# The first two head pairs of an attention stage scored straight from an fp32 projection, with the operand stacks of that block written by one queue

## What is computed

```python
qkv = x @ w_qkv.T                    # x is layer-normalised, 16 heads of 8 channels
q, k, v = (_split_heads(t) for t in jnp.split(qkv, 3, axis=-1))
L = jnp.einsum('bhqd,bhkd->bhqk', q, k) * scale
k_y = _split_heads(x @ w_ky.T)
L_y = jnp.einsum('bhqd,bhkd->bhqk', q, k_y) * scale
agg = jnp.sum(jnp.exp(jnp.clip(L_y, -15.0, 15.0)) * mask, axis=-1, keepdims=True) + EPS
r = jnp.log(jnp.abs(L) + EPS) - jnp.log(agg + EPS)
w = jax.nn.softplus(r) * mask
A = w / (jnp.sum(w, axis=-1, keepdims=True) + EPS)
out = jnp.einsum('bhqk,bhkd->bhqd', A, v)     # then the output projection and the residual
```

## Time before, and the profile of one execution

| | us |
|---|---|
| median of 3 executions | 423.61 |
| lowest and highest | 421.04, 424.43 |
| span of the profiled execution | 421.1 |

### The profile page before, as it was taken

One profiled execution on the slowest core, in us unless ns is written; L12 is line 12 of the kernel. 1 busy time (PEld: TensorE's weight loads), 2 busy tenths in 40 slices (PEclk: granted clock), 3 DMA queues, 4 the chain that ended last, 5 costly groups with the idle time before them and its releaser, 6 DMA issues.

```text
span 421.1 us, 8327 instructions
## 1 busy us (share of the span) xinstructions
PE 330.0 (78%) x2412; PEld 195.9 (47%) x2412; DVE 304.9 (72%) x628; ACT 297.8 (71%) x866; POOL 149.6 (36%) x252
## 2 busy tenths in 40 slices
PE   6878899995766435778788677777978996889992
PEld 6638899752233111222334223242333473589992
DVE  5653443378899969999999999988999657444431
ACT  2915456424999979999999989996777646345561
POOL 5575544400443560021411214112530016654452
PEclk9989999996699655876958969878998989899997
DMA  8775666134478996001200012000300274666540
GB/s 248 263 222 153 199 162 173 46 107 138 133 203 224 220 243 134 0 2 38 64 0 2 0 39 63 2 2 0 101 0 2 66 264 121 189 189 180 166 134 26
DMA packets 37993, 47.61 MB, mean 113 GB/s; under 512 B 4288, under 2 KB 26816, under 8 KB 37696
## 3 DMA queue, kind: packets, MB, share of 16 engines
q1 hardware_dynamic: 33616, 36.20, 31.7%
q0 software_dynamic: 2560, 6.30, 5.3%
q10 hardware_dynamic: 1776, 4.60, 3.3%
HBM read 24.02 MB, written 6.29 MB: 72 GB/s over the span
## 4 chain that ended last, share of the span: by engine, by line
ACT 34%; PE 33%; DVE 13%; issue 6%; DMA 4%; POOL 3%; SPq 2%; DVEq 1%; another core or an unknown queue 1%; ACTq 1%; POOLq 0%
ACT R L944 14%; PE PS L1522 9%; ACT R L952 9%; PE PS L1532 8%; ACT CL L944 7%; PE PS L1667 3%; PE PS L1451 3%; PE PS L1475 2%; SPq L463 2%; DVE R L1296 2%; DVE R L1281 2%; DMA QPS<-R 2%; PE PS L1649 2%; DVE R L1027 1%; ACT R L969 1%
## 5 line engine op out<-in xcount | busy, mean ns | idle before, releaser
L1296 DVE TENSOR_TENSOR R<-PS,MB 128x1024 int32<-128x1024 int32 (+1 forms) x96 | 97.9, 1034 | 13.3 <-PE PS L1649 13.1
L836 ACT ACTIVATE R<-PS,R 128x128 f32<-128x128 f32 x184 | 52.6, 368 | 49.1 <-PE PS L1522 23.8
L952 ACT ACTIVATE R<-R 128x1024 f32<-128x1024 f32 x64 | 80.0, 1261 | 9.7 <-DVE R L1296 9.6
L944 ACT ACTIVATE R<-R 128x384 f32<-128x384 f32 (+2 forms) x192 | 77.1, 411 | 3.1 <-DVE R L1281 3.1
L1634 PE MATMUL PS<-R 64*128 64x512 bf16 (+3 forms) x256 | 40.1, 367 | 33.7 <-DVE CL L1281 16.3
L1281 DVE SCALAR_TENSOR_TENSOR R<-PS,MA 128x1024 f32<-128x1024 f32 x64 | 59.5, 946 | 1.1 <-PE PS L1634 1.1
L1667 PE MATMUL PS<-R,V 128*32 128x256 f32 (+3 forms) x512 | 56.3, 526 | 3.6 <-ACT R L952 3.5
L1522 PE MATMUL PS<-R 128*128 (+1 forms) x368 | 51.7, 283 | 6.2 <-DVE R L1162 4.5
L1649 PE MATMUL PS<-QPS,R 64*128 64x512 bf16 (+3 forms) x256 | 38.2, 349 | 15.5 <-DVE R L1281 8.4
L1522 PEld LDWEIGHTS PS<-R 128*128 128x128 f32 x368 | 44.6, 191 | 10.2 <-issue 8.5
L1532 PE MATMUL PS<-R 128*128 (+1 forms) x368 | 48.8, 276 | 0.7 <-ACT R L836 0.7
(11 more groups left out here) (184 smaller groups left out, 460.8 us busy)
## 6 DMA issues: line engine op xcount, KB each, us to landing
R<-w SPq DMA_DIRECT2D x38, 258.0 KB
R<-R SPq DMA_DIRECT2D x32, 128.0 KB, 2.4
R<-R SPq DMA_DIRECT2D x16, 256.0 KB, 7.9
QPS<-R SPq DMA_DIRECT2D x32, 128.0 KB, 2.4
R<-w ACTq DMA_DIRECT2D x8, 258.0 KB
rows_d<-X SPq DMA_DIRECT2D x8, 256.0 KB, 3.9
R<-w ACTq DMA_DIRECT2D x1, 2048.0 KB, 8.3
rows_d<-R SPq DMA_DIRECT2D x8, 256.0 KB, 2.4
```

Of the source, the lines that this page charges most:

```text
L836: last = act.activation(HT[:, k % 2, c * P:(c + 1) * P], PS[:, k % 2, c * P:(c + 1) * P], ACT.Gelu, bias=W1[:, k, F + c:F + c + 1])
L944: act.activation(e, e, ACT.Exp, scale=SCALE, accum_out=aggf[:, ds(s + (2 * i + par) * STEPS, 1)])\
L952: act.activation(w, w, ACT.Ln, bias=1.0, scale=1.0).then_inc(s_ln, 1)
L1296: dve.tensor_tensor(weights(v)[:, :, at:at + n].bitcast(i32), PS[:, SLOTS[slot(b_fill(v, g))], 0:n].bitcast(i32), spread(mask, 1, 2), ALU. ...
```

## The change

**Direct scores.** Two more projections of block 0, with weights WS, give queries and `k_y` keys of the first four head pairs' worth of rows spaced so that head (pair, parity) has its 8 rows at partition 0, 32, 64 or 96. WS is cleared by POOL and filled from WA in the first expert layer, where WH was made. ScalarE copies the queries out of PSUM (`direct_queries`), VectorE the keys (`direct_keys`), both in fp32, into FS, and steps 0 and 1 (DIRECT = 2) are scored by fp32 matmuls with 8 rows instead of bf16 ones with 64. TensorE waits at step 0 for these two copies and for the stacks only at step 2.

**Stacks.** WH, `half_stack` and `first_keys` go; the first two stacks are written whole by SyncE, 16 DMAs of 128 KB, in the order first terms, second terms, third terms.

**Engines.** The second terms of m = 0 and 1 go from ScalarE to POOL. The normalised rows of blocks 1 to 3 go from VectorE to POOL (`middle_rows`, 12 instructions), with most of their inverse deviations. The copies of the turned blocks 1 to 3 go from ScalarE to VectorE.

**Order.** Projection 2 goes behind step 1, 3 inside step 2, 4 behind step 2, then one a step (`PROJECT_AT`); the turns of blocks 1, 2, 3 behind steps 1, 3, 4 (`TURNS_AT`), with banks 7, 7, 7; the token-major rows t = 0 to 7 behind steps 1, 2, 3, 5, 5, 6, 7, 7 (`ROWS_AT`). On VectorE remainders, copies and `value_rows` stand between the clips of a step (`between`), not behind them. On POOL terms of m = s + 1 are made in step s, where it was s + 2.

```diff
+DIRECT = 2
+FIRST_BANK = (6, 7)
+PROJECT_AT = (None, None, 1, None, 2, 3, 4, 5, 6, 7, 8, 9)
+ROWS_AT = (1, 2, 3, 5, 5, 6, 7, 7)
+TURNS_AT = {1: 1, 2: 3, 3: 4}
-TURN_BANK = ((0, 1, 0, 1), (0, 1, 0, 7), (7, 7, 0, 1))
+TURN_BANK = ((0, 1, 0, 1), (0, 7, 7, 7), (7, 7, 0, 1))
...
-            half_stack(0, 0)
-            half_stack(1, 0, (2,))
-            for i in range(2):
-                half_stack(i, 1)
+            for term in range(TERMS):
+                for i in range(2):
+                    stack(i, (term,))
...
+            def middle_rows(b):
+                for n in range(b * TB, (b + 1) * TB):
+                    pool.tensor_scalar(XN2[:, n, :], X[:, n, :], mv[:, n, 0:1], lnt[:, 2, n:n + 1],
+                                       ALU.subtract, ALU.mult).then_inc(s_xn, 1)
...
-                m = s - 1 + FIRST_PROJECTIONS
-                if s == 1:
-                    second_term(2)
-                    third_term(2)
-                if 0 < s < A_AT:
+                m = s + 1
+                for k in {1: (2,), 3: (3, 4)}.get(s, (m,) if 3 < s < A_AT else ()):
+                    second_term(k)
+                    third_term(k)
+                if s == A_AT:
                     second_term(m)
-                    third_term(m)
-                elif s == A_AT:
-                    second_term(m)
-                elif s == R_AT:
+                elif s in (R_AT, Q_AT):
                     third_term(m - 1)
                     second_term(m)
-                elif s == Q_AT:
+                elif s == Q_AT + 1:
                     third_term(m - 1)
                     second_term(m)
                     third_term(m)
...
+                if s == 2 and g == 0:
+                    remainder(2)
+                if s == 3 and g < 2:
+                    remainder(3 + g)
+                if g == 0 and 4 <= s < len(PROJECTIONS) - 1:
+                    remainder(s + 1)
+                for b in range(1, NB):
+                    if g == 0 and s == TURNS_AT[b] + 1:
+                        copy_xnt(b)
+                for t in range(NT // 2):
+                    if s == ROWS_AT[t] + 1 and g == (2 if t in (4, 7, 1) else 1):
+                        value_rows(t)
...
+            def bank_read(t):
+                pe.wait_ge(s_qc, t + 1)
+                pe.wait_ge(s_vc, 2 * t + 2)
...
+                if k == 1 and g == 2:
+                    bank_read(1)
+                if k == 1 and g == 3:
+                    pe.wait_ge(s_xnt, NB + 3)
...
+            def direct_projections():
+                for w in range(2):
+                    pe.matmul(PS[:, FIRST_BANK[w], :], WS[:, w, :], XNT2[:, 0:SEQ],
+                              start=True, stop=True).then_inc(s_pe, 1)
...
-                if b == NB - 1:
+                if b:
+                    pe.wait_ge(s_xnt, NB + b + 1)
...
+                        if s < DIRECT:
+                            rows = slice(QUAD * (s % 2 * 2 + par), QUAD * (s % 2 * 2 + par) + HD)
+                            last = pe.matmul(to, FS[rows, 0, i * P:(i + 1) * P],
+                                             FS[rows, 1, 0:(i + 1) * P], start=True, stop=True)
```

More of the change, by code:

```diff
@@ L355, in build @@
         s_den = sem("denominators_summed")
+        s_ilin = sem("middle_inverse_deviation_begun")
         s_linv = sem("last_inverse_deviation_begun")
@@ L756, in normalise @@
                                    ALU.mult).then_inc(s_num, 1)
+            def middle_rows(b):
+                for n in range(b * TB, (b + 1) * TB):
+                    pool.tensor_scalar(XN2[:, n, :], X[:, n, :], mv[:, n, 0:1], lnt[:, 2, n:n + 1],
+                                       ALU.subtract, ALU.mult).then_inc(s_xn, 1)
+            var, inv, tmp = (lnt[:, k, TB:] for k in (0, 2, 3))
+            pool.wait_ge(s_ilin, 1)
+            link(pool.tensor_tensor(tmp, inv, inv, ALU.mult))
+            link(pool.tensor_tensor(tmp, tmp, var, ALU.mult))
+            link(pool.tensor_scalar(tmp, tmp, -0.5, 1.5, ALU.mult, ALU.add))
+            link(pool.tensor_tensor(inv, inv, tmp, ALU.mult))
+            for m in range(2):
+                second_term(m)
+            for b in range(1, NB):
+                middle_rows(b)
             for s in range(END_STEP):
@@ L1265, in _ @@
             variance(3)
-            remainder(0)
-            inverse(3)
-            remainder(1)
-            for m in range(2):
-                last_term(m)
-            normal_rows(3, XN2)
+            direct_keys()
+            dve.wait_ge(s_std, 4)
+            dve.reciprocal(lnt[:, 2, TB:], lnt[:, 1, TB:]).then_inc(s_ilin, 1)
             def clip_scores(s, g):
@@ L1344, in after @@
                         scaled_q_terms(b)
-                m = s - 1 + FIRST_PROJECTIONS
-                if s == 1:
-                    remainder(2)
-                    dve.wait_ge(s_c, 9)
-                    for t in range(FIRST_ROWS):
-                        v_rows(t)
-                if s and m < len(PROJECTIONS):
-                    remainder(m)
-                if FIRST_ROWS < s <= NT // 2:
-                    v_rows(s - 1)
                 for b in range(NB):
@@ L1385, in between @@
             def between(s, g):
+                if s == 0 and g < 2:
+                    remainder(g)
+                if s == 0 and g == 2:
+                    for m in range(2):
+                        last_term(m)
+                if s == 2 and g == 0:
[4 more added lines that the diff above has]
+                    remainder(s + 1)
+                for b in range(1, NB):
+                    if g == 0 and s == TURNS_AT[b] + 1:
+                        copy_xnt(b)
+                for t in range(NT // 2):
+                    if s == ROWS_AT[t] + 1 and g == (2 if t in (4, 7, 1) else 1):
+                        value_rows(t)
                 for b in range(NB):
@@ L1605, in _ @@
             pe.wait_ge(s_xnt, NB + 1)
-            pe.wait_ge(s_wh, 2)
+            pe.wait_ge(s_wsp, 2)
+            direct_projections()
             for m in range(2):
                 project(m)
-            for t in range(FIRST_ROWS):
-                q_v_rows(t)
-            project(2)
-            for b in range(1, NB - 1):
-                turn(1, b)
-            pe.wait_ge(s_xnt, 2 * NB - 1)
-            pe.wait_ge(s_c, 9)
+            pe.wait_ge(s_c, 8)
             def slot_free(n):
@@ L1701, in after @@
             def after(s):
-                if s != 1 and s + FIRST_PROJECTIONS < len(PROJECTIONS):
-                    project(s + FIRST_PROJECTIONS)
-                if s == 2:
-                    pe.wait_ge(s_qc, 2)
-                    pe.wait_ge(s_vc, 4)
-                    turn(1, NB - 1)
-                if FIRST_ROWS <= s < NT // 2:
-                    q_v_rows(s)
+                for m in range(2, len(PROJECTIONS)):
+                    if s == PROJECT_AT[m]:
+                        project(m)
+                for b in range(1, NB):
+                    if s == TURNS_AT[b]:
+                        turn(1, b)
+                for t in range(NT // 2):
+                    if s == ROWS_AT[t]:
+                        q_v_rows(t)
                 if s == NT // 2 + 1:
-                    pe.wait_ge(s_qc, NT // 2)
-                    pe.wait_ge(s_vc, NT)
+                    bank_read(NT // 2 - 2)
+                    bank_read(NT // 2 - 1)
                 for b in range(NB):
@@ L1742, in _ @@
                 if s == 0:
-                    for i in range(2):
-                        pe.wait_ge(s_stk0[i], STACK_DMAS)
-                if s == HP // 2:
+                    pe.wait_ge(s_eq, 1)
+                    pe.wait_ge(s_ek, 1)
+                if s == DIRECT:
                     for i in range(2):
```

111 lines of the change are left out of this document (52 added, 59 removed).

## The result

| | before | changed |
|---|---|---|
| median of the runs, us | 422.53 (421.04 to 424.43, 4 runs) | 434.15 (433.17 to 438.08, 4 runs) |
| span of the profiled execution, us | 421.1 | 432.6 |
| first turn of block 0 in it, us | 89.62 | 91.45 |

The ratio is 1.0294, with a 95% interval of 1.0252 to 1.0337: about 12 us slower, where 433.0 (425 to 440) and "slower" with 0.85 were forecast. The forecast stood on a median of 423.6 for the kernel before; one more execution brought that to 422.53. As a difference, 9.4 us were forecast and 11.6 measured.

The account below looks back on a forecast made before the run. ScalarE's gapless 4.36 us steps, after a fixed chain to step 0, were taken to bound the kernel. Step 2 came earlier, later waits outweighed it: +9.5 at the second logarithm, 433 us, range 425 to 440.

Parts of the forecast that it names:

- Step 0: Start of the attention: with direct fp32 scores, step 0's exponentials start at 97.4, 6.1 us earlier.
- Step 2: Its start waits for the 16 stack DMAs, landing at 107.8: 109.4 to 109.6 instead of 112.9.
- Step 2 to 3: Projection 3 waits for VectorE's copy of block 1, projections 3 and 4 at half clock: 8.1 us.
- 3 to 4: VectorE's remainders, clips and value rows 1 hold up the turn of block 2: 6.8 us.
- 4 to 5 and 5 to 6: Remainder and copy delay clip 1, 5.3 us; then remainder 6, copy, projection 7 and token-major rows, 5.9 us.
- rival 1: TensorE stays at 1.2 GHz longer: +13.3 (437) through step 4, +21 (444) through step 7; chance 0.17.
- 6 to 9: Steps of 5.0, 5.0 and 5.1 us, with clip 1 late and two query rows in the first two.
- 9 to 12: Remainders 10 and 11 wait for POOL's third terms; step 9 at 150.6, step 10 at 157.8, step 11 at 163.9.
- The idle time before the first logarithm: ScalarE's old idle of 2.11 us there goes, since the scaled queries land while ScalarE is still busy.
- Rival 2: Only the two remainders behind POOL's new order cost, steps 2 to 8 keeping 4.36 us: +1.7, 425; chance 0.10.
- rival 4: The fp32 scores take the time the stacks took, leaving step 2 where it was: 436; chance 0.03.
- Rival 3: Faster: issue time hides, stacks land by 105.5, step 2 follows step 1 at 106.6: 417.3; chance 0.05.

Follow-up runs that it names:

- e10: Changed kernel with the edits of e1, e7 and e8 together (POOL order, ScalarE copies, VectorE work behind the third clip); 427.84 us, ratio 1.0125 to the kernel before.
- e2: Changed kernel plus idle bf16 products on TensorE in steps 0 to 2, meant to keep its clock up; ratio 1.0307 to the kernel before.
- e7: Changed kernel with the copies of turned blocks 1 to 3 given back from VectorE to ScalarE; ratio 1.0195 to the kernel before.
- e6: As e4, without the idle products of steps 0 and 1 and with projection 11 behind the turn of the scaled queries; ratio 0.996 to the kernel before.
- e1: Changed kernel with only POOL's order around the last two remainders altered, terms made earlier; ratio 1.0195 to the kernel before.
- e11: As e6, but the first turned scaled queries go to PSUM bank 6 instead of 7; ratio 0.9943 to the kernel before.
- e9: Changed kernel with the edits of e1 and e7 together; 426.90 us, ratio 1.0084 to the kernel before.
- e8: Changed kernel with VectorE's remainders and value rows put behind the third clip, copies left between clips; ratio 1.0345 to the kernel before.
- e4: Changed kernel's start plus idle products in steps 0 and 1, with later work back in the old kind of order, a step ahead; ratio 1.0017 to the kernel before.
- e3: Changed kernel with both the idle products of e2 and the POOL order of e1; ratio 1.0305 to the kernel before.

## Why the prediction came out as it did

The mechanism was right in nearly every step, and the sum of the stage was 2.3 us short: +9.5 forecast at the second logarithm, +11.8 measured. That 433.0 and 434.15 lie only 1.2 us apart owes something to luck: the base of the forecast was 1.1 us higher than the median that it was compared with. And the forecast let the shift go through to the end, where the profiled executions give back 1.8 us behind the last exponentials. By its own steps:

- **Step 0.** Forecast 97.4, that is 7.8 behind the turn; measured 7.56. The unknown price of the fp32 scores was put at 1.0 us for 512 columns, which makes 2.5 for a step; a step's 16 passes took 1.99 + 0.70 us at full clock and 4.78 at half. Right.
- **Step 2.** Forecast 109.4 to 109.6, 19.8 to 20.0 behind the turn, bound by the stacks; measured 20.64. The reason held, by a hair. The last of the 16 DMAs was issued 10.0 us after the first, where 9.75 was taken, and landed 2.3 to 2.6 us later, where 2.1 was taken; that is most of the 0.8 us. TensorE waited only 0.24 us for it, because the clock had fallen at about 100.2, while step 0 ran, and not in the idle time behind step 1 as forecast: all of step 1's work on TensorE went at half clock and ended at 110.11. That the landing bound the step shows in e10, where TensorE was done 0.5 us sooner, stood still for 0.72 us and began the scores at the same 18.90 us behind the turn:

```profile
108.69 0.61 PE L1663 MATMUL PS<-R 64*128 64x512 bf16 x6 [0.72 <-issue]
```

- **Step 2 to 3.** 8.1 forecast, 7.78 measured, with the copy, the idle TensorE (2.41) and projection 3 behind it in the order given. e2 (6.19 at full clock) and e7 (5.36 with the copy gone) confirm both halves.
- **3 to 4.** 6.8 forecast, 6.53 measured.
- **4 to 5 and 5 to 6.** 5.3 and 5.9 forecast, 6.04 and 7.47 measured. This is the term that was too small, by 2.3 us together. The sum had full clock from here on, since the old trace had it from 113 on the earlier trace rows; in the changed kernel it fell again. Projection 6 took 2.05 us, projection 7 1.46, and the two sets of token-major rows 3.26 where 3.0 was meant to hold them and projection 7. Stretches of the changed kernel, columns as above:

```profile
126.00:128.00 2.00, 0.57 (x3) 0.41 (x4) 2.00 (x4) 1.34 (x4) 0.89 (x2) 0.88 0.78 208
128.00:130.00 2.00, 2.00 (x5) 0.86 (x5) 1.69 (x4) 1.27 (x6) 0.88 (x1) 0.50 0.74 199
130.00:133.00 3.00, 1.61 (x11) 0.54 (x9) 1.82 (x3) 2.29 (x11) 0.00 (x0) 0.84 0.74 200
133.00:138.00 5.00, 4.25 (x10) 2.86 (x10) 2.33 (x4) 4.01 (x18) 1.77 (x2) 0.66 0.43 120
```

  It is rival 1 in part: not half clock through step 7, but in three stretches of it, about 114 to 117, 127.5 to 131 and 134.5 to 138. That TensorE's new gaps let it fall is what the runs suggest (with e6's order it stays full from step 2 to step 9), not a thing that one of them isolates.
- **6 to 9.** 5.0, 5.0 and 5.1 forecast; 4.94, 5.15, 4.85 measured. Clip 1 comes 0.5, 0.5 and 0.3 us late for ScalarE there; the second set of query rows in step 7 and 0.33 us ahead of step 9's first exponential are most of the rest.
- **9 to 12.** 7.2 and 6.1 forecast, 7.25 and 6.24 measured, with VectorE idle for 2.38 and 2.00 us where 2.2 and 2.0 were expected. The idle time before the first logarithm is gone, as forecast. e1 shows that the order was worth 3.5 us.
- **Rival 2** (only the two remainders cost) and **rival 4** (the fp32 scores eat the gain of step 0) are out: rival 2 by the table, rival 4 by step 0 at 7.56. **Rival 3** (faster) named the wrong condition. It wanted the stacks down at 105.5, with the rest of the order as the change has it. What makes this start pay is the order of the steps (e6, e11), and then it pays 0.4 to 0.6%. With earlier stacks and the new order TensorE's half clock would have held step 2 to within 0.24 us all the same.

What the forecast missed as an idea: it priced each in-step wait for itself, at one clock. Two terms do add up (e1 and e7 in e9). The others aren't independent: moving VectorE's work back alone gave nothing up to step 8 (e8), on top of e9 it gave nothing either (e10), and with TensorE's schedule moved back as well all of the loss up to step 9 was gone (e4, e6). TensorE's schedule moved back alone was not tried, so what share of the loss is its own stays open.

## To carry to other kernels

Where engines hand work round inside a step, make each piece a full step before it is used. With all pieces so, steps 3 to 9 took 4.36 us with an earlier and with a later start alike; with some made in the step that uses them, steps 2 to 9 took 4.6 to 9.4 us. The runs show this for the whole order (e4, e6), and single waits of this kind for the copy (e7), the bank of the token-major rows (e8) and the remainder (e10); that the rule holds piece by piece they don't show. Before you put a gain ahead of a pipeline, ask what stands first behind it: here 6.3 us gained at step 0 were 1.3 to 2.6 at step 2, because the stacks and TensorE at half clock, 0.24 us apart in the changed kernel, were the next bounds. When a wait is removed, look for the next thing that lands: e11 took away 1.8 us at step 9 to 10 and got none of it at the logarithm, because the queries' DMA ended last.

## What the runs showed of the hardware

**The granted clock fell although TensorE was busy.** Stretches of e4, where idle products filled TensorE's gaps behind the direct scores, and of e6, where they didn't (columns as above). e4:

```profile
92.00:95.80 3.80, 3.80 (x20) 1.49 (x19) 2.38 (x4) 3.02 (x6) 1.23 (x5) 1.00 0.20 50
95.80:98.00 2.20, 2.20 (x8) 0.75 (x8) 2.20 (x4) 1.81 (x10) 1.15 (x3) 0.50 0.68 177
```

e6:

```profile
98.00:100.00 2.00, 1.06 (x10) 0.47 (x6) 2.00 (x3) 1.23 (x5) 0.47 (x1) 0.98 0.41 104
100.00:105.00 5.00, 4.42 (x16) 2.31 (x16) 4.64 (x7) 3.56 (x17) 3.95 (x5) 0.50 0.72 194
```

The times of a fall are worked out from the mean clock of stretches of 1 us. In e4 it went from 2.4 to 1.2 GHz 8.7 us behind the first turn, with TensorE busy 3.80 of the last 3.80 us; in e6 8.8 us behind it, with 1.06 of the last 2.00. What e4 did in the time ahead of the fall was mostly fp32 passes of 8 rows with one or two idle products between them. The time of the fall is not a property of the kernel: two executions of the kernel before had it 9.0 and 10.3 us behind the turn, e2 and e3, with the same instructions up to there, 9.1 and 12.7, all others between 8.3 and 10.7. So in this kernel a busy TensorE in the profile was no sign that the clock would hold (e2, e3, e4), and a few idle products didn't keep it up in e2 and e4; ends of matmuls are modelled in the profile, so "busy" is itself not exact. The Trainium skill (TensorE: Matmul & The Clock Gate, "HAM oscillation — how this bites in real kernels") blames gaps in which the engine is idle. The kernel before agrees with that (busy 0.93 of 3.00 us ahead of its fall), e6 hardly, with gaps of 0.49 and 1.03 us, e4 does not. Whether more or wider products would have held the clock was not tried.

**The 8-row fp32 pass.** 16 passes of one step's scores took 4.78 us at 1.2 GHz and 2.69 (1.99 + 0.70) at 2.4 GHz.

**POOL's `tensor_scalar` with two pointers** on 128x128 fp32: 12 in 10.31 us, 0.86 each, against the 0.85 that was taken between the bounds.
